# Int8 attention on one core: maxima scaled by the activation engine, waits for own rounds, and constant products behind the scores

## The reference

```python
def _fq(x, delta, zp, n_bits):
    xi = _round_ste(x / delta) + zp
    xq = jnp.clip(xi, 0.0, 2.0 ** n_bits - 1.0)
    return (xq - zp) * delta

def _attn(x, ctx, wq, wk, wv, wo, bo, dq, dk, dv, dw):
    ...
    sim = jnp.einsum('bhid,bhjd->bhij', _fq(q, dq, 128.0, 8), _fq(k, dk, 128.0, 8)) * SCALE
    attn = jax.nn.softmax(sim, axis=-1)
    out = jnp.einsum('bhij,bhjd->bhid', _fq(attn, dw, 0.0, 8), _fq(v, dv, 128.0, 8))
    ...
    return out @ wo + bo
```

## Time and profile before

| | us |
|---|---|
| median of 3 runs | 1045.59 |
| lowest, highest | 1045.52, 1046.74 |
| the profiled execution | 1047.26 |
| its span, first to last instruction | 1045.5 |

### The profile page before, as it was taken

One profiled execution on the slowest core, in us unless ns is written; L12 is line 12 of the kernel. 1 busy time (PEld: TensorE's weight loads), 2 busy tenths in 40 slices (PEclk: granted clock), 3 DMA queues, 4 the chain that ended last, 5 costly groups with the idle time before them and its releaser, 6 DMA issues.

```text
span 1045.5 us, 23536 instructions
## 1 busy us (share of the span) xinstructions
PE 869.4 (83%) x8314; PEld 530.6 (51%) x8314; DVE 762.1 (73%) x1680; ACT 612.3 (59%) x1487; POOL 519.7 (50%) x1045
## 2 busy tenths in 40 slices
PE   3798988974555878998998899998988788888895
PEld 1344444443333545555755456565555466565664
DVE  4888888978775655665566766677476788989886
ACT  0877777858885213554355456664555566666674
POOL 2677777875553424763444556655344322323313
PEclk9999556555555989999999899999999999999998
DMA  9400000000000000000000010000000000000000
GB/s 263 154 1 2 0 0 1 2 1 0 1 2 1 1 0 1 2 2 2 1 2 2 24 25 22 24 23 14 2 1 2 1 1 2 2 12 0 10 2 21
DMA packets 23573, 16.39 MB, mean 16 GB/s; under 512 B 8744, under 2 KB 20400, under 8 KB 23344
## 3 DMA queue, kind: packets, MB, share of 16 engines
q1 hardware_dynamic: 23472, 15.06, 5.0%
HBM read 10.85 MB, written 1.05 MB: 11 GB/s over the span
## 4 chain that ended last, share of the span: by engine, by line
PE 50%; DVE 26%; ACT 10%; issue 8%; POOL 4%; DMA 1%; DVEq 1%; SPq 0%; ACTq 0%; POOLq 0%
ACT sb_E L1243 6%; PE ps_context L784 5%; DVE sb_neg_raw L1542 4%; PE ps_context L787 3%; PE ps_scores L860 3%; DVE sb_E L1970 3%; PE ps_scores L884 3%; DVE sb_inv_den L1785 2%; POOL sb_E L2267 2%; PE ps_scores L676 2%; PE ps_scores L737 2%; PE ps_scores L777 2%; PE ps_turned L1088 2%; DVE sb_neg_half L1753 2%; PE ps_turned L698 2%
## 5 line engine op out<-in xcount | busy, mean ns | idle before, releaser
L1243 ACT ACTIVATE sb_E<-ps_scores,sb_neg_max,sb_score_scale 128x256 f32<-128x256 f32 (+1 forms) x384 | 190.9, 515 | 60.0 <-DVE sb_neg_max L1545 59.6
L2267 POOL TENSOR_SCALAR sb_E<-sb_E,sb_inv_sum 128x256 f16<-128x256 f32 x256 | 123.5, 482 | 43.4 <-DVE sb_inv_sum L1582 25.3
L1496 ACT ACTIVATE sb_E<-ps_scores,sb_ff_bias 128x512 f32<-128x512 f32 x128 | 87.6, 688 | 66.6 <-PE ps_scores L1129 64.2
L1146 PE MATMUL ps_turned<-sb_moe_down,sb_E 128*128 128x128 f16 x512 | 92.6, 220 | 23.9 <-DVE sb_E L1970 23.8
L1970 DVE TENSOR_TENSOR sb_E<-sb_E 128x512 f16<-128x512 f32 x128 | 93.1, 745 | 23.4 <-ACT sb_E L1499 21.2
L1753 DVE TENSOR_REDUCE sb_neg_half<-ps_scores 128x16 f32<-128x1024 f32 x48 | 58.7, 1222 | 68.3 <-PE ps_scores L860 68.3
L1542 DVE TENSOR_REDUCE sb_neg_raw<-ps_scores 128x4 f32<-128x1024 f32 (+1 forms) x80 | 97.3, 1217 | 13.4 <-PE ps_scores L676 11.7
L1565 DVE TENSOR_REDUCE sb_neg_quad<-ps_scores 128x2 f32<-128x512 f32 (+1 forms) x96 | 64.5, 686 | 42.0 <-PE ps_scores L739 30.0
L1148 PE MATMUL ps_turned<-sb_moe_down,sb_E 128*128 128x128 f16 x512 | 92.1, 219 | 0.0
L1147 PE MATMUL ps_turned<-sb_moe_down,sb_E 128*128 128x128 f16 x512 | 92.1, 219 | 0.0
L2202 POOL TENSOR_SCALAR sb_veps<-sb_mv 128x2 f32<-128x2 f32 x72 | 17.4, 241 | 149.0 <-DVE sb_mv L1525 144.7
(11 more groups left out here) (285 smaller groups left out, 2260.5 us busy)
## 6 DMA issues: line engine op xcount, KB each, us to landing
sb_moe_up<-in_moe_up SPq DMA_DIRECT2D x1, 2048.0 KB
sb_KS<-sb_qk_parts SPq DMA_DIRECT2D x96, 16.0 KB, 1.8
sb_QS<-sb_qk_parts SPq DMA_DIRECT2D x96, 16.0 KB, 1.8
sb_rows<-in_rows SPq DMA_DIRECT2D x1, 1216.0 KB, 7.8
out_x<-sb_raw_context SPq DMA_DIRECT2D x8, 128.0 KB, 1.8
sb_X<-in_x SPq DMA_DIRECT2D x1, 768.0 KB, 9.9
sb_square<-in_square SPq DMA_DIRECT2D x1, 768.0 KB, 11.0
sb_ctxT<-in_ctxT SPq DMA_DIRECT2D x1, 512.0 KB, 11.2
```

The costliest lines, as they stand in the source:

```text
L1146: pe.matmul(dst, u_hi, hi, start=(first and i == 0), stop=False, skip_group_check=True)
L1243: last = act.activation(E[:, ring, head], SC[t % 2][:, head], ACT.Exp, bias=neg_max[:, ring, h:h + 1], scale=scale, accum_out=row_sum[:, r ...
L1496: last = act.activation(U_full[:, k % 4, :], banks[k % 4], ACT.Gelu, bias=bias, scale=1 / WEIGHT_SCALE)
L2267: last = pool.tensor_scalar(E16[:, ring, SEQ * h:SEQ * h + SEQ], E[:, ring, SEQ * h:SEQ * h + SEQ], inv_sum[:, ring, h:h + 1], HALF, ALU.m ...
```

## The change

Three edits. First, in A1 the reduce itself negates the maximum, and ACT multiplies it by the score scale with an activation of 128x4 elements ahead of the exponentials, and waits for that through a new semaphore `scaled_max`; DVE's scaling and its wait for the reduce are gone. A2's maxima are as they were. Second, in both attentions the first scores of a batch wait for the rounds up to the one that made their own Q and K, one batch of steps earlier, instead of all rounds before. Third, in every step of A1, ahead of the first unit and behind the last one too, PE issues two products (steps with a round) or four (steps without) behind the scores: the 16-bit identity times itself, repeated four times, 128x512, written into the bank that the step's turn overwrites. Nothing reads the result.

```diff
@@ counts
-             keyed=NBATCH, raw_max=n, exped_half=n)
+             keyed=NBATCH, exped_half=n)
+    c["scaled_max" if layer.over_self else "raw_max"] = n
@@ quant_scores
-                    wait(pe, S["round_free"], B["round_free"] + L.rounds_before(p, t))
+                    wait(pe, S["round_free"], B["round_free"] + L.rounds_before(p, t - L.per_batch + 1))
@@ block.tensor
+            def keep_clock(t, count):
+
+                for i in range(count):
+                    pe.matmul(TP[t % 2][:, :], ident16[:, :], ident16[:, None, :].to_broadcast([P, 4, P]), start=True,
+                              stop=True)
@@ quant_step of PE
                 quant_scores(L, B, p, t)
+                if L is A1:
+                    keep_clock(t, 2 if n_rounds > 0 else 4)
                 if n_rounds > 0:
                     round_of(L, B, p, t, 0)
@@ quant_exps
                 act.wait_ge(S["maxed"], B["maxed"] + n + 1)
+                if L.over_self:
+                    act.activation(neg_max[:, ring, 0:L.heads], neg_raw[:, ring, 0:L.heads], ACT.Copy, scale=score_scale[:, 0:1])\
+                       .then_inc(S["scaled_max"], 1)
                 used = "normed" if L.over_self else "rounded"
                 wait(act, S[used], B[used] + n - 3)
+                if L.over_self:
+                    act.wait_ge(S["scaled_max"], B["scaled_max"] + n + 1)
@@ quant_maxima
-                dve.tensor_reduce(neg_raw[:, ring, 0:L.heads], src, AX.X, ALU.max).then_inc(S["raw_max"], 1)
-                dve.wait_ge(S["raw_max"], B["raw_max"] + n + 1)
-                biased, layer = (L.heads, 0) if L.over_self else (BIASED, 1)
-                dve.tensor_scalar(neg_max[:, ring, 0:biased], neg_raw[:, ring, 0:biased],
-                                  neg_scale[:, layer:layer + 1], None, ALU.mult).then_inc(S["maxed"], 1)
-                if not L.over_self:
+                if L.over_self:
+                    dve.tensor_reduce(neg_raw[:, ring, 0:L.heads], src, AX.X, ALU.max, negate=True)\
+                       .then_inc(S["maxed"], 1)
+                else:
+                    dve.tensor_reduce(neg_raw[:, ring, 0:L.heads], src, AX.X, ALU.max).then_inc(S["raw_max"], 1)
+                    dve.wait_ge(S["raw_max"], B["raw_max"] + n + 1)
+                    dve.tensor_scalar(neg_max[:, ring, 0:BIASED], neg_raw[:, ring, 0:BIASED], neg_scale[:, 1:2], None,
+                                      ALU.mult).then_inc(S["maxed"], 1)
```

## The result

| | before | after |
|---|---|---|
| median of 4 runs each, us | 1045.55 | 1031.41 |
| lowest, highest | 1044.49, 1046.74 | 1031.12, 1036.71 |
| the profiled execution | 1047.26 | 1031.33 |
| its span | 1045.5 | 1029.5 |

The ratio is 0.9873, 95% interval [0.9845, 0.9901]: the changed kernel is faster by 14.1 us in the medians and by 15.9 us in the profiled executions.

What follows compares the result with a forecast made beforehand. No engine was taken as full: a chain round PE (at the low clock), DVE and ACT bounds A1. Gains 16.0 + 1.9 + 1.2 + 0.8 + 1.0 less 2.3 and 1.0 make 17.6 us, 1045.6 to 1028.0; range 1018 to 1043.

Steps and rivals of the forecast that it cites:

- likeliest case: The forecast itself: an A1 batch between 21.5 and 22.8 us, time 1022 to 1034 us, chance 0.52.
- head, to the first maximum: Start of A1: products ahead of the first turn and first scores delay it, 2.3 us lost (0 to 6).
- batch 0: First batch of A1, bound by ACT: from 22.8 to 20.9 us, 1.9 us gained.
- batches 1 to 5: Middle of A1: each batch falls from 25.2 to 22.0 us, 3.2 gained (1.6 to 4.5), 16.0 in all.
- batch 7: Last batch of A1, which has no Q/K round: 0.8 us gained.
- seam, last maximum of A1 to first scores of A2: Between the attentions: 22 more products nearly cancel against work halved by the raised clock, 1.0 us lost (0 to 5).
- A2, first scores to last maximum: Second attention: maxima at most 0.15 us sooner in seven or eight batches, 1.0 us gained in all.
- stays up: A1: with the products the clock rises in the head and stays high; PE's load becomes 18.2 us a batch.
- The first: Rival in A1: clock rises and falls by turns; 1038 us at a low share of 0.15, chance 0.15.
- The second rival: In A1 the clock stays low and PE's 33.4 us a batch become the period; 1127 us, chance 0.06.
- The third: Rival in A1: ACT replaces PE, copy and wait cost 0.6 us a unit, batch 23.6; 1037.5 us, chance 0.10.
- The fourth: Rival: DVE and ACT interlock better, head hides its products, batch 21.2 us; 1021.6 us, chance 0.14.

Runs made afterwards that it cites:

- waits_only: Part 2 alone on the kernel before: a batch's first scores wait for their own rounds only; 1038.00 us, ratio 0.9922.
- after_again: The changed kernel run once more, unaltered, on one chip beside three variants of it; 1033.64 us (1029.32 to 1035.94).
- short_head: The changed kernel without the products in the twelve first steps ahead of A1's first live unit; 1028.12 us, ratio 0.9817.
- products_only: Part 3 alone on the kernel before: constant products in A1, scaling on DVE and waits as before; 1052.29 us, ratio 1.0047.
- old_waits: Parts 1 and 3: the changed kernel with a batch's first scores waiting for all rounds again; median 1057.58 us (1037.47 to 1064.82).
- quarter_rows: The changed kernel with its products over 32 rows instead of 128, same number and length; 1076.64 us, ratio 1.0304.
- copy_twice: The changed kernel with a second, unused 128x4 activation on ACT ahead of the first; 1044.71 us (1040.91 to 1050.16).
- scale_by_vector: Parts 2 and 3: the changed kernel with DVE scaling the maxima as before; 1038.10 us, ratio 0.9935.

## Why the prediction was right, and where its terms were not

The predicted median was 1028.0, the measured one 1031.4, in the range and in the likeliest case; the sum was 17.6 us for the profiled execution and it came to 15.9. Term by term, from the starts of the maxima (before, after, in the profiled executions; by the spans the sum is 16.0):

| term | predicted | measured |
|---|---|---|
| head, to the first maximum (24.00, 25.38) | -2.3 | -1.4 |
| batch 0 (22.72, 23.01) | +1.9 | -0.3 |
| batches 1 to 5 (25.20, 21.97 each) | +16.0 | +16.2 |
| batch 6 (23.2, 21.4) | +1.2 | +1.8 |
| batch 7 (19.0, 19.4) | +0.8 | -0.4 |
| seam, last maximum of A1 to first scores of A2 | -1.0 | -0.2 |
| A2, first scores to last maximum (89.1, 88.1) | +1.0 | +1.0 |
| rest | 0 | -0.7 |

**Part 1.** DVE's saving was read rightly. ACT's price was not: 0.39 us a unit where 0.30 was taken, because the prediction gave the wait for its own result 0.05 us and it is 0.20. Nor does the way from the maximum's end to the first exponential stay as long as it was: it grew from 0.31 to 0.42 us. The fullest engine was named rightly, but that the gain in batches 1 to 5 came out within 0.2 us is partly luck, since two errors cancel: ACT's bound is 18.3 + 8 x 0.39 = 21.4 us and not 20.7, and the batch of 22.0 stands 0.6 above it and not 1.3. Where the cancelling fails it shows: in batch 7, which was to gain 0.8 us and lost 0.4, ACT is busy 18.75 of 19.41 us. DVE's idle time is as forecast in kind (it waits for exponentials at the inversion), 2.6 us a batch where 1.7 were counted. The Trainium skill (ScalarE: Activation LUTs, Rules for kernel authors) budgets about 0.3 us for an activation, and the trace agrees for the instruction (298 ns in the mean). The pace and the wait, 0.19 and 0.20 us, had to be measured from starts.

**Part 2.** Right in size (1.0 us of the 1.20 a batch appears when it is alone) and in what comes next. What the prediction did not see is its second use: it keeps the clock up. Products with the old waits gave 1057.6 us. A2's gain came as forecast and is this part's own: from its first maximum to its last A2 took 88.4 us in before, 87.7 in after and 87.6 in waits_only.

**Part 3.** The clock rose in the head and stayed through batches 1 to 6, as taken, and PE's load there is 18.9 us a batch (18.2 forecast). The step that failed is "stays up" ahead of and behind them. In batch 0 of after it fell at 29.7 us, right behind the first of these two waits of PE for the first units' exponentials,

```profile
29.57 0.47 PE L677 MATMUL ps_scores<-sb_KBD,sb_QS 32*128 32x512 f16 x1 [1.40 <-ACT sb_E L1257]
30.66 0.60 PE L677 MATMUL ps_scores<-sb_KBD,sb_QS 32*128 32x512 f16 x1 [0.62 <-ACT sb_E L1257]
31.19 1.89 PE L705 MATMUL ps_turned<-sb_ident 128*128 128x512 f16 x4
```

and then the products, twice as long there (1.89 us for four), kept PE full until it rose at 39.9 us. The forecast gain of batch 0, 1.9 us, turned into a loss of 0.3. The dip can account for that: against after_again and short_head, batch 0 changes by 0.2 to 0.26 us for each microsecond at the low level inside it, so 10.2 us are worth some 1.9 to 2.7 us, an estimate from these three traces. At the end of batch 7 it fell again, at 197.0 us, 1.8 us behind a pause of 1.66 us, and stayed low for 6.8; only 2 us of that lie in batch 7. In the head the first 24 products took 6.79 us (7.3 estimated) and held up the turn of z by 2.8 us (3.4 estimated); by the first scores 1.8 us were left, by the first maximum 1.4.

**The rivals.** The first, a clock that rises and falls by turns, is not what the changed kernel does in its middle, but it is what its third part does alone, at the price of its formula. The rule of the Trainium skill (TensorE: Matmul & The Clock Gate, A second HAM failure mode: psum-queue depth-cycling), that small pauses of PE between groups let the clock swing, agrees with products_only (mean clock 0.81) and old_waits, and in after with the two dips, but not with batches 1 to 6 of after: there PE pauses 1.22 us once in each batch and 0.71 us once, and the clock stays at 1.00. The second rival comes true in part where the products load a quarter of the array, as quarter_rows shows. The third, ACT at 0.60 a unit, was the right mechanism at too high a price: copy_twice, with 0.58 us from the first copy to the exponentials, takes 23.2 us a batch in batches 2 to 6 (23.6 in the rival). The fourth did not occur; short_head reached 1028 by the head and batch 0, its other batches are as long as in after.

## What to carry to other kernels

Filler work (products whose result nobody reads) that is to keep the tensor engine's clock up was worth here what the pauses beside it allowed: take the waits at the seams away first, then add the products, and count their price at the low level, since that is paid wherever the clock falls. Put none where another engine's first result waits behind them. A scaling moved to another engine costs there not only its own time but the wait for its result, which on ACT here was as long again.

## What the runs showed of the hardware that was not expected

- The parts don't add up. By the medians of the table, part 1 was worth -2 us alone, -2.8 on part 2 and +6.7 on parts 2 and 3 (nearly all of it in one dip of the clock in the last batch, by the two traces); part 3 was worth -6 alone and +9.4 on parts 1 and 2.
- PE busy 97% with 32-row products stayed at the low level, PE busy 86% (81% in copy_twice) with products over 128 rows at the high one. It fell behind pauses of 0.95 and 1.41 us (products_only), of 0.41 and 1.16 (old_waits, in three batches) and of 0.65 and 0.31 (scale_by_vector), and stayed up through 1.22 in each batch of after and through 1.39 and 0.84 in copy_twice. So the length of a pause alone does not tell; what else does is not shown.
- Products over 32 rows ran side by side with score products over 32 rows, with starts 0.01 us apart (quarter_rows).
- The same kernel's executions differ by 5 to 7 us (after, after_again); where two of them were looked into, most of the difference was the length of one dip of the clock from batch 0 on, 10.2 or 23.9 us. With the wait for hT at the head of batches they differ by 27 us (old_waits).
- An activation of 128x4 elements is listed with 0.30 us; one behind it that does not need its result starts 0.19 us after it, one that does 0.39 us after it (medians over 48 units of copy_twice and 52 of after).
- The granted clock shown ahead of a trace's first change of it isn't to be relied on: waits_only shows 1.00 up to 218 us at the pace of the low level, and its four executions, all within 0.8 us of each other, are listed with mean clocks of 0.856 to 0.939.
